# Grouped convolution by three half-width products per column pair, with a shared product copied inside PSUM

## The reference, cut to what matters

```
x = x + ffn0(cond0(x))
x = x + ffn1(conv1(x))

cond0: agg_w[b] = sum_k att[b,k] * weight[k]       (64x64 per example, att from a small MLP)
       out = agg_w[b] @ x[b] + agg_b[b]
ffn0:  out = x @ (A @ B.T).T + bias                (rank 128)
conv1: out = grouped conv over positions, 9 taps, 4 groups of 16 channels, pad 4,
       + ctx[b, channel] + bias[channel]
ffn1:  out = x @ W_up.T + (LoRA of rank 8 of the expert with the largest gate logit)
```

## Time and profile before

| | |
|---|---|
| median of the runs | 1254.97 us |
| the profiled execution's own time | 1255.82 us |
| its span, first to last instruction | 1254.1 us |
| mean granted TensorE clock | 0.984 of full speed |
| PE busy | 1207.6 us |
| DVE busy | 621.1 us |
| ACT busy | 292.5 us |
| POOL busy | 318.5 us |

### The profile page before, as it was taken

The page is one execution under the profiler, slowest core; times in us unless marked ns, Lnnn a source line. Parts: engine busy times, 40 slices in busy tenths (PEclk is TensorE's granted clock), DMA queues, the critical chain, the costliest instruction groups (busy, mean ns, idle before and its releaser), DMA issues.

```text
span 1254.1 us, 17453 instructions
## 1 busy us (share of the span) xinstructions
PE 1207.6 (96%) x7114; PEld 1073.5 (86%) x7114; DVE 621.1 (50%) x1271; ACT 292.5 (23%) x422; POOL 318.5 (25%) x120
## 2 busy tenths in 40 slices
PE   5578999999999999999999999999999999999998
PEld 5457889889888988988898888889888988998888
DVE  7663544544544455444454545444455444445542
ACT  4522221222222122222212222221222222222110
POOL 6413312222331222233122223322222332222000
PEclk9678999999999999999999999999999999999999
DMA  6713544443344434434444433455434344543311
GB/s 224 210 55 74 138 139 117 102 128 107 110 135 140 128 97 119 111 111 132 139 135 97 116 111 109 131 140 135 106 106 125 99 127 139 138 106 103 78 41 51
DMA packets 104073, 147.61 MB, mean 118 GB/s; under 512 B 12098, under 2 KB 81858, under 8 KB 99874
## 3 DMA queue, kind: packets, MB, share of 16 engines
q1 hardware_dynamic: 103994, 146.49, 42.0%
HBM read 79.04 MB, written 33.59 MB: 90 GB/s over the span
## 4 chain that ended last, share of the span: by engine, by line
PE 92%; DVE 5%; SPq 1%; DMA 1%; issue 0%; ACT 0%; POOL 0%; DVEq 0%
PE O L736 58%; PE F L721 14%; PE F L702 7%; PE F L666 2%; PE F L667 2%; PE O L755 2%; PE F L668 2%; DVE Wl L541 1%; SPq L196 1%; DVE aggT L536 1%; PE O L747 1%; PE F L683 1%; PE F L684 0%; DVE wks L531 0%; DMA wkr<-in_wkx_dram 0%
## 5 line engine op out<-in xcount | busy, mean ns | idle before, releaser
L736 PE MATMUL O<-Wh,yh 128*128 128x292 f32 (+2 forms) x1536 | 509.1, 331 | 0.0
L736 PE MATMUL O<-Wl,yh 128*128 128x292 f32 (+2 forms) x1536 | 497.8, 324 | 0.0
L736 PE MATMUL O<-Wh,yl 128*128 128x292 f32 (+2 forms) x1536 | 497.6, 324 | 0.0
L262 POOL TENSOR_TENSOR x<-x,biasb 128x1032 f32<-128x1032 f32 x64 | 157.3, 2460 | 638.6 <-DMA x<-in_xP_dram 638.6
L736 PEld LDWEIGHTS O<-Wh,yh 128*128 128x128 f32 x1536 | 290.2, 189 | 29.6
L736 PEld LDWEIGHTS O<-Wl,yh 128*128 128x128 f32 x1536 | 290.6, 189 | 24.6
L736 PEld LDWEIGHTS O<-Wh,yl 128*128 128x128 f32 x1536 | 289.6, 189 | 22.2
L254 POOL TENSOR_TENSOR xTl<-xTr,xTh 128x2048 fp32r<-128x2048 f32 x32 | 149.9, 4684 | 193.3 <-ACT xTh L307 193.3
L483 DVE STREAM_TRANSPOSE yr<-F 128x512 f32<-128x512 f32 x128 | 91.6, 716 | 165.4 <-PE F L721 165.4
L307 ACT ACTIVATE yh<-yr 128x1024 fp32r<-128x1024 f32 x64 | 67.8, 1060 | 442.7 <-DVE yr L483 442.7
L525 DVE TENSOR_TENSOR osb<-O,x 128x256 f32<-128x256 f32 (+1 forms) x192 | 98.0, 510 | 139.5 <-PE O L755 135.8
(11 more groups left out here) (119 smaller groups left out, 1184.5 us busy)
## 6 DMA issues: line engine op xcount, KB each, us to landing
x<-in_xP_dram SPq DMA_DIRECT2D x64, 516.0 KB, 6.0
Xlo<-x SPq DMA_DIRECT2D x512, 64.5 KB, 2.7
xTr<-in_xT_dram SPq DMA_DIRECT2D x32, 1024.0 KB, 4.9
out_dram<-osb SPq DMA_DIRECT2D x64, 512.0 KB, 3.3
Wr<-in_Wd_dram SPq DMA_DIRECT2D x8, 530.0 KB, 11.5
agb<-agb_scratch SPq DMA_DIRECT2D x32, 128.0 KB, 2.9
biasb<-in_biasP_dram SPq DMA_DIRECT2D x1, 516.0 KB, 10.3
Br<-in_Bd_dram SPq DMA_DIRECT2D x1, 512.0 KB, 6.4
```

Source lines behind the costliest of these rows:

```text
L262: pool.tensor_tensor(x1[:, t % XR], x1[:, t % XR], biasb[:, :, :], ALU.add).then_inc(g_xb, 1)
L736: last = pe.matmul(O[c][:, 0:w_], w[:, t % YR, k, :], m[:, k, c0:c0 + w_], start=k == 0 and n_ == 0, stop=k == 7 and n_ == 2)
```

## The change

The convolution of a tile is computed in another way. For neighbouring even and odd columns the two blocks of band matrices T0 and T1 act on raw columns a, b and c (at 2i, 2i+1 and 2i+2). The even output T0·a + T1·b equals T0·(a − b) + (T0 + T1)·b, and the odd output T0·b + T1·c equals T1·(c − b) + (T0 + T1)·b. The product (T0 + T1)·b is shared.

- `unit_p(s, g)` makes the shared product: three matmuls of 256 columns into F[4]. ACT's `pc(s, g)` copies it twice into F[g]. `unit_c(s, g)` then adds six matmuls of 256 columns into F[g] without clearing it. That is nine matmuls of 256 columns in place of six of 512, with ACT's copy between the two units.
- `xd(s, q)` on DVE makes the differences a − b and c − b (two tensor_tensor of 512 elements), and ACT's and DVE's `xs` become two instructions each (512 and 1024 elements).
- One raw buffer Xr serves both halves q, so `rx(s, q)` waits until DVE's `xs` of the half before has ended (semaphore v_xs).
- The y buffer has three slots in place of four. v and u share memory. `ut` waits for `v_vl`. `unit_u` waits for the copies of the slab before.
- In the loop the orders change: `unit_p(it+1, g)` goes behind steps 16, 18, 22 and 26. ACT does pc(it+1, 0) and pc(it+1, 1) ahead of txh(it+3), and xs(it+2, 0) ahead of ys(it+1, 1). DVE has xd(it+2, 0) behind f(t, 2), xs(it+2, 0) between the last two ty, and xd(it+2, 1) ahead of the last f.
- `zc` computes the gate logits in another way, with one more small operation in its chain, and the table lgb goes.

The diff, cut to its core (semaphore numbers of zc, memory overlays and the matching changes to the layout of inputs are left out):

```diff
-YR = 4
+YR = 3
@@ SP
             def rx(s, q):
-                if s > 0:
-                    sp.wait_ge(p_c, 4 * (s - 1) + 2 * q + 2)
                 sp.wait_ge(v_x1, 4 * s + 2 * q + 2)
+                if s + q > 0:
+                    sp.wait_ge(v_xs, 2 * s + q)
                 for g in range(2):
                     for b in range(4):
-                        sp.dma_start(Xlo[:, 2 * q + g, b, :].bitcast(fp32), x1[p0:p0 + 16, (2 * s + q) % XR, :, :]).then_inc(d_rx[q], 16)
+                        sp.dma_start(Xr[:, 4 * g + b, :], x1[p0:p0 + 16, (2 * s + q) % XR, :, :]).then_inc(d_rx[q], 16)
@@ ACT
             def xs(s, q):
-                act.wait_ge(d_rx[q], 128 * (s + 1))
-                copy(Xhi[:, 2 * q:2 * q + 2], Xlo[:, 2 * q:2 * q + 2].bitcast(fp32)).then_inc(a_xs, 1)
+                act.wait_ge(v_d, 2 * s + q + 1)
+                copy(Xh[:, q, 2], Xr[:, :, 1:128:2])
+                copy(Xh[:, q, 0:2], Xd[:, q, 0:2]).then_inc(a_xs, 1)
+            def pc(s, g):
+                act.wait_ge(p_p, 4 * s + g + 1)
+                if s == 0:
+                    act.wait_ge(v_x1, g + 1)
+                elif s + 1 < NS:
+                    act.wait_ge(v_x1, 4 * (s + 1) + g + 1)
+                else:
+                    act.wait_ge(v_ty, 4 * (s - 1) + g + 1)
+                copy(F[g][:, :].rearrange("p (b e i) -> p b e i", b=4, e=2),
+                     F[4][:, 0:256].rearrange("p (b i) -> p b i", b=4).unsqueeze(2).broadcast_to([128, 4, 2, 64])).then_inc(a_pc, 1)
@@ ACT, loop
                 zt(2 * it)
+                pc(it + 1, 0)
+                pc(it + 1, 1)
                 txh(it + 3)
+                pc(it + 1, 2)
                 ys(it + 1, 0)
+                pc(it + 1, 3)
+                xs(it + 2, 0)
                 ys(it + 1, 1)
-                xs(it + 2, 0)
                 zt(2 * it + 1)
@@ DVE
+            def xd(s, q):
+                dve.wait_ge(d_rx[q], 128 * (s + 1))
+                if s > 0:
+                    dve.wait_ge(p_c, 4 * (s - 1) + 2 * q + 2)
+                dve.tensor_tensor(Xd[:, q, 0], Xr[:, :, 0:128:2], Xr[:, :, 1:128:2], ALU.subtract)
+                dve.tensor_tensor(Xd[:, q, 1], Xr[:, :, 2:129:2], Xr[:, :, 1:128:2], ALU.subtract).then_inc(v_d, 1)
             def xs(s, q):
                 dve.wait_ge(a_xs, 2 * s + q + 1)
-                dve.tensor_tensor(Xlo[:, part], Xlo[:, part].bitcast(fp32), Xhi[:, part].bitcast(fp32), ALU.subtract).then_inc(v_xs, 1)
+                dve.tensor_tensor(Xl[:, q, 2], Xr[:, :, 1:128:2], Xh[:, q, 2].bitcast(fp32), ALU.subtract)
+                dve.tensor_tensor(Xl[:, q, 0:2], Xd[:, q, 0:2], Xh[:, q, 0:2].bitcast(fp32), ALU.subtract).then_inc(v_xs, 1)
@@ DVE, loop
                 ty(it + 1, 0)
                 ty(it + 1, 1)
                 f(t, 2)
+                xd(it + 2, 0)
                 ys(it + 1, 0)
                 ty(it + 1, 2)
+                xs(it + 2, 0)
                 ty(it + 1, 3)
                 zc(t + 1)
                 ys(it + 1, 1)
-                xs(it + 2, 0)
                 f(t + 1, 0)
                 f(t + 1, 1)
+                xd(it + 2, 1)
                 f(t + 1, 2)
@@ TensorE
             def unit_u(s):
+                    pe.wait_ge(a_pc, 4 * max(s - 1, 1))
+            def unit_p(s, g):
+                if g % 2 == 0:
+                    pe.wait_ge(v_xs, 2 * s + g // 2 + 1)
+                if g == 0:
+                    pe.wait_ge(v_v, min(s + 2, NS) if s > 0 else 1)
+                else:
+                    pe.wait_ge(a_pc, 4 * s + g)
+                b0 = 4 * (g % 2)
+                for n_, (w, m) in enumerate(((Th, Xh), (Tl, Xh), (Th, Xl))):
+                    last = pe.matmul(F[4][:, 0:256], w[:, g, 2, :], m[:, g // 2, 2, b0:b0 + 4, :].rearrange("p b i -> p (b i)"),
+                                     start=n_ == 0, stop=n_ == 2)
+                last.then_inc(p_p, 1)
             def unit_c(s, g):
-                for blk in range(2):
-                    for n_, (w, m) in enumerate(((Th, Xhi), (Tl, Xhi), (Th, Xlo))):
-                        last = pe.matmul(F[g][:, :], w[:, g, blk, :], m[:, g, :, blk:blk + 128],
-                                         start=blk == 0 and n_ == 0, stop=blk == 1 and n_ == 2)
+                pe.wait_ge(a_pc, 4 * s + g + 1)
+                b0 = 4 * (g % 2)
+                dst = F[g][:, :].rearrange("p (b e i) -> p e b i", b=4, e=2)
+                for e in range(2):
+                    for n_, (w, m) in enumerate(((Th, Xh), (Tl, Xh), (Th, Xl))):
+                        last = pe.matmul(dst[:, e], w[:, g, e, :], m[:, g // 2, e, b0:b0 + 4, :],
+                                         start=False, stop=n_ == 2, skip_group_check=True)
                 last.then_inc(p_c, 1)
@@ TensorE, loop
                     if n in (18, 21, 26, 30):
                         unit_c(it + 1, {18: 0, 21: 1, 26: 2, 30: 3}[n])
+                    if n in (16, 18, 22, 26):
+                        unit_p(it + 1, {16: 0, 18: 1, 22: 2, 26: 3}[n])
```

More of the change, by code:

```diff
@@ L81, in adaln_ffn @@
         agb = sb("agb", [128, 256])
-        v = sb("v", [128, 256])
+        v = over("v", "u", [128, 256])
         vh = sb("vh", [128, 2, 2, 4, 16], f32r)
@@ L85, in adaln_ffn @@
         x1 = sb("x1", [128, XR, 8, 129])
-        Xlo = sb("Xlo", [128, NG, 4, 129], f32r)
-        Xhi = sb("Xhi", [128, NG, 4, 129], f32r)
+        Xr = sb("Xr", [128, 8, 129])
+        Xl = sb("Xl", [128, 2, 3, 8, 64], f32r)
+        Xd = over("Xd", "Xl", [128, 2, 3, 8, 64])
+        Xh = sb("Xh", [128, 2, 3, 8, 64], f32r)
         yh = sb("yh", [128, YR, 8, 128], f32r)
@@ L102, in adaln_ffn @@
         F = [ctx.enter_context(nc.psum_tensor(f"F{i}", [128, 512], fp32)) for i in range(5)]
-        small = over("small", "Xhi", [128, 1024])
+        small = over("small", "Xh", [128, 1024])
         pack = small[:, 0:402]
@@ L123, in adaln_ffn @@
         Bsum = small[:, 832:960]
[L124 to L132, removed]
+        ats = over("ats", "Xh", [128, 24], 1024)
+        atsT = over("atsT", "Xh", [24, 128], 1056, f32r)
+        bkr = over("bkr", "Xh", [24, C], 1184)
+        bks = over("bks", "Xh", [24, C], 1184, f32r)
+        bkh = over("bkh", "Xh", [24, C], 1248, f32r)
+        wkr = over("wkr", "yh", [24, C * C + C])
+        wks = over("wks", "yh", [24, C * C + C], 0, f32r)
+        wkh = over("wkh", "Xr", [24, C * C], 0, f32r)
+        ccX = over("ccX", "yl", [128, 2, 4, 2, 4, 16], 1088)
+        onesr = over("onesr", "yl", [128, 128], 2112, f32r)
         Lr = over("Lr", "x1", [96, L], 5 * 8 * 129)
@@ L318, in ut @@
                 act.wait_ge(p_u, s + 1)
+                if s > 0:
+                    act.wait_ge(v_vl, s)
                 copy(u[:, :], F[4][:, 0:256]).then_inc(a_u, 1)
@@ L495, in zc @@
                 dve.wait_ge(p_cc, 3 * t + 1)
[L496 to L500, removed]
+                dve.scalar_tensor_tensor(out=zl[:, :], in0=gsB[:, :], scalar=cbn[:, t // 2, t % 2:t % 2 + 1], in1=O[0][:, 0:36],
+                                         op0=ALU.mult, op1=ALU.add).then_inc(v_z, 1)
                 if t > 0:
@@ L583, in _ @@
             dve.tensor_tensor(Al[:, :, :], Ar[:, :, :], Ah[:, :, :].bitcast(fp32), ALU.subtract).then_inc(v_a, 1)
+            dve.wait_ge(d_t, 16)
+            dve.tensor_tensor(Tr[:, :, 2, :], Tr[:, :, 0, :], Tr[:, :, 1, :], ALU.add).then_inc(v_t, 1)
             dve.wait_ge(d_fs, 16)
@@ L597, in _ @@
                 addx(0, i)
-            for k in range(6):
+            for k in range(5):
                 w(k)
+            xd(0, 0)
+            w(5)
             xs(0, 0)
@@ L621, in _ @@
             dve.wait_ge(d_eb, 16)
-            for e in range(E):
-                dve.tensor_scalar(lgb[:, :, e], cbf, gsB[:, e:e + 1], ebb[:, e:e + 1], ALU.mult, ALU.add).then_inc(v_ws, 1)
             for i in range(4):
                 addx(1, i)
+            xd(1, 0)
             xs(1, 0)
-            dve.wait_ge(v_ws, 8)
+            xd(1, 1)
             dve.wait_ge(v_cb, 5)
@@ L704, in unit_o @@
                 last.then_inc(p_o, 1)
-            def unit_c(s, g):
+            def unit_p(s, g):
                 if s >= NS:
@@ L821, in _ @@
             for g in range(4):
+                unit_p(0, g)
                 unit_c(0, g)
@@ L859, in laid_out @@
     pos = np.array([[8 * a + (r + 4) % 8 for a in range(128)] for r in range(8)])
-    row = np.array([[8 * (32 * (k // 2) + p % 32) + 2 * (p // 32) + k % 2 for k in range(8)] for p in range(128)])
+    row = np.array([[8 * (2 * (32 * (k // 2 % 2) + p % 32) + k // 4) + 2 * (p // 32) + k % 2 for k in range(8)] for p in range(128)])
     xT = x.reshape(NS, 256, 8, 128).transpose(0, 3, 2, 1)
```

65 lines of the change are left out of this document (38 added, 27 removed).

## The result

The changed kernel takes 1452.99 us (median of 4 runs, 1449.41 to 1454.5), against 1254.3 us (1253.12 to 1255.6) for the kernel before, run beside it. The ratio is 1.158, with a 95% interval of 1.1554 to 1.1605. The forecast was 1445.

The account below looks back on a forecast made before the run. PE's own work was taken as the bound, busy 96% of the span. The sum was 1255.8 + 176.9 (29 periods at +6.1) − 1.2 + 14.4 = 1445.9, less 0.85: 1445 us, range 1245 to 1500.

Parts of the forecast that it names:

- Matmuls: PE's convolution: a group costs 1.065 us instead of 1.40, so −1.34 us for each slab.
- strips: Rival at unit_c: PSUM writes in 64-column runs make matmuls twice as long, about 1500 us; chance 0.03.
- The copy: ACT's pc between unit_p and unit_c: takes 0.6 us and makes group 0 wait, +0.24 us a period (0 to 0.7).
- Where `txl` lands: On POOL: the copies ahead of txh move txl to offset 19.45 to 24.1, where DVE comes to xd.
- The wait at the second `unit_zt`: PE waits for zc, late because txl and xb hold DVE: 5.3 us a period (3.2 to 6.5).
- xd is not held: Rival: DVE's xd runs beside POOL, PE waits 0.5 us, 1251 us; chance 0.10.
- only txl blocks: Rival: xb falls outside the chain or the clock holds, 2.1 to 3.1 us a period, 1330 to 1360 us; chance 0.15.
- all hidden: Rival: PE finds every result ready, so only the matmuls count, 1217 to 1227 us; chance 0.12.
- The clock: PE at half clock behind each recurring wait: +1.9 us a period (0 to 2.5).
- Strided reads at no cost: xd and xs reading every second element of Xr: no extra time, about 1 us at the upper end.
- The start: Slab 0 waits, added DVE work ahead of the loop and the shared raw buffer: +14 us (5 to 20).
- The tail: The last two convolutions, which lack txl: −0.6 us each.

Follow-up runs that it names:

- experiment 6: Changed kernel with txh ahead of pc, two POOL waits delaying xb, and DVE's 1024-element part of xs moved behind zc(t+1): 1230.53 us, ratio 0.9812.
- Experiments 1: Changed kernel with ACT's txh(it+3) moved back ahead of pc(it+1, 0): 1312.0 us, ratio 1.0476 to the kernel before.
- experiment 3: Changed kernel with POOL's txl in the loop replaced by a memset of xTl to zero, which reads no SBUF: 1313.11 us, ratio 1.0479.
- 4: Changed kernel with POOL's xb cut to one element per partition from tile 5 on: 1352.84 us, ratio 1.0788.
- 5: Changed kernel with txh ahead of pc and two POOL waits putting xb behind DVE's vlo and second ys: 1251.07 us, ratio 0.9979.
- experiment 7: Kernel of experiment 6 with, in the first iteration only, DVE's xd(1, 1) and both engines' xs(1, 1) moved later: 1225.72 us, ratio 0.977.
- experiment 8: Changed kernel with 40 unused 256-column matmuls added ahead of the second unit_zt of each period: 1394.66 us, ratio 1.1118.

## Why the prediction was right

- **Matmuls, −1.34 us a period.** Borne out. In experiment 6, where nothing waits, the period is 1.22 us shorter, which with the copy's +0.24 is a little more than forecast. The matmuls that write strips start 0.12 us apart, like others of 256 columns (starts at 650.72, 650.84 and 650.96 below), so the rival "strips" falls.

```profile
650.26 0.28 PE L793 MATMUL O<-Wh,yl 128*128 128x256 f32 x1
650.50 0.38 PE L778 MATMUL F<-Xh,Th 128*128 128x256 f32 x1
650.72 0.28 PE L778 MATMUL F<-Xh,Tl 128*128 128x256 f32 x1
650.84 0.28 PE L778 MATMUL F<-Xl,Th 128*128 128x256 f32 x1
650.96 0.28 PE L778 MATMUL F<-Xh,Th 128*128 128x256 f32 x1
```

- **The copy, +0.24 us a period.** The copy took 0.58 us where I took 0.6. The two distances in front of and behind 650.50 in the lines above are 0.24 and 0.22 in place of 0.12 each: 0.22 us.
- **Where `txl` lands.** I forecast 19.45 to 24.1, and it ran from 19.54 to 24.16. That the data for `xd` are there at 20.3 didn't follow from my own figures (12.5 + 5.3 + 2.7 = 20.5); in this period `xd` starts at 20.24 without a wait. ACT's timeline has `txh` right behind the second copy, as walked:

```profile
651.86 0.58 ACT L310 ACTIVATE F<-F 128x512 f32<-128x512 f32 x1 [1.41 <-PE F L766]
652.47 1.91 ACT L310 ACTIVATE xTh<-xTr 128x2048 fp32r<-128x2048 f32 x1
```

- **The wait at the second `unit_zt`, 5.3 us.** PE waits 5.08 us in 23 periods and 4.47 in 6, 4.95 on average, and each step of the walk stood within about 0.4 us of its forecast: `xd` 20.24 to 25.30 (forecast 20.3 to 25.3), `xb` until 27.6 (27.7), `zc`'s end 33.34 (33.65). The two kinds are those of the forecast, which had the chain 0.64 us shorter where `xb` runs beside a transpose; 0.61 was measured. Against experiment 6, in which PE doesn't wait, `unit_zt` starts 5.30 us later (offset 33.40 against 28.10). Experiments 1, 3 and 4 remove its parts one at a time, and 5 all but 0.21 us of it. The rivals "xd is not held", "only txl blocks" and "all hidden" fall with that. The last describes what experiment 7 reaches: 1217 to 1227 us was its forecast, 1225.72 came, and it takes timed POOL operations, a moved `xs` and another order in it = 0 to get there. One reading was loose: of the nine operations of `zc` that I set against the 2.31 us, two read the PSUM tile O and the casts have one operand. The time of the chain stands.
- **The clock, +1.9 us a period.** 1.9 by experiment 8. The terms close to within 0.3 us: the period is 1.22 us below the kernel before where nothing waits (experiment 6), the late `unit_zt` adds 5.30, or 5.2 with the six shorter ones, and what is left of the measured +6.14 is 2.2. I had picked 1.9 inside 0 to 2.5 from a single row, so that it lies this close is partly luck.
- **Strided reads at no cost.** The second `xd` (L506) takes 0.68 us for 512 elements at a step of two, against 0.69 for a plain operation of 512 in the earlier trace rows. What hung on the Trainium skill's "Advanced Engine Details and Errata", section SBUF Cachelines, holds: this trace agrees with it.
- **The start, +14.4 us, was too small by 6.** Counted with the period of it = 0 the forecast was 20.5 us, and 26.4 came. The part with the shared raw buffer was right (it = 0: +14.5, forecast +15.9). The failing term is what I gave slab 0 and the additional DVE work ahead of the loop: 4.6 us, measured 11.9. (By its own parts, 3.6 − 1.34 + 2.2, that term is 4.5.) In slab 0 PE waits 2.77 and three times 0.67 us between p and c, 4.8 us where I had 3.6; its waits in front of L837, for the low part of the per-example weights, grew from 16.3 to 18.9 us, and its wait for `txl` at `unit_u` of it = 0 from 1.7 to 3.2. A part is the clock, which the forecast had at nothing here: experiment 8 has the same start, and there `unit_u` of it = 0 comes at 106.00 and not at 109.90. The mean granted clock up to that point is 0.80 in the changed kernel and 0.84 in experiment 8 (the lines below, in this order; the kernel before has 0.83). So about 3.9 of the 11.9 us come and go with the clock where the code is the same, and about 8 stay, against 4.6. The rest of the miss isn't split up.

```profile
0.00:109.90 109.90, 61.45 (x270) 52.45 (x270) 69.92 (x78) 43.86 (x63) 42.70 (x33) 0.80 0.46 143
```

```profile
0.00:106.00 106.00, 58.17 (x271) 49.38 (x271) 69.86 (x78) 43.85 (x63) 42.33 (x33) 0.84 0.48 149
```

- **The tail** gave −1.9 where −1.2 was forecast.

The total lies close because the loop carries 172 of the 196.5 us and the terms of its period came within 0.3 us. The start did not: its miss of 6 us is nearly the whole distance between the forecast of 1445 and 1453.

## What to carry to other kernels

Two short copies put ahead of what triggers another engine cost 141 us here, while the two added waits and one moved line that brought all 202 back remove no work at all: before an order is changed, draw when every POOL operation will run and which DVE operations with two SBUF operands it will then lie beside. A held operation looks busy in a profile, so compare each group's mean with the same shape elsewhere before believing that an engine has become the bound. And price a recurring PE wait with the half clock behind it: here a `unit_zt` that comes 5.3 us late makes the period 7.4 us longer than in experiment 6 (42.57 against 35.21).

## What the runs showed of the hardware

- In these runs DVE operations with two SBUF operands and POOL's tensor_tensor, which reads SBUF, exclude each other instruction by instruction, whichever starts second is held, and its recorded duration contains the holding: `xd` 4.46 us in place of 0.68, `ys` 4.79 in place of 1.22, POOL's `xb` 3.30 in place of 2.42, and a conversion of three elements 1.62. A POOL memset of the same tile, which only writes, held nothing (experiment 3). The Trainium skill, "SBUF — State Buffer", section Who interferes with whom, states the same split between POOL instructions that read and those that only write; experiment 3 agrees, with 0.68 us beside the memset. It also counts copies and casts, under conditions on their operands that no run here tests, among what can collide; the cast of three elements with its 1.62 us agrees.
- The gains aren't additive. Without `txl` in the way 141 us come back, without `xb` 100, and with both timed 202, 39 less than their sum. PE's waits at `unit_zt` are nearly additive (they fell by 86.5, 58.7 and 138 us), so the overlap is mostly in what the clock costs: by the mean granted clocks (0.928, then 0.966, 0.960 and 0.977) the time at half clock falls by 119, 101 and 151 us, and half of 119 + 101 − 151 is 34.
- An idle PE is dearer than a PE with useless work: 40 additional matmuls in each of 29 periods made the kernel 58 us faster, about 54 of them in the periods it = 1 to 28.
- The Trainium skill, "PSUM — Partial Sum Buffer", table of specifications, says that any non-contiguous pattern slows matmuls significantly. Runs of 64 columns with gaps of 64 did not: 0.12 us a matmul, as for contiguous ones.
- An ACT copy of 512 elements from PSUM into PSUM, each source element read twice, took 0.58 us, like one into SBUF (0.593 in the earlier trace rows, on 3 partitions).
